# Decoder block on one core: last normalisations of the attention stage moved between engines, scan matmuls reordered

## The reference

```python
x = layernorm(x + mixer(x))          # linear recurrence with a gate
x = layernorm(x + attention(x, ctx)) # 16 heads of 16
x = layernorm(x + experts(x))        # 8 experts, each takes its top 256 tokens

def mixer(x):
    u = x @ W_in + b_in                       # 64 states
    h_t = h_{t-1} @ A + u_t @ Bm              # over 1024 steps
    y = (hs @ C.T + u @ D.T) * sigmoid(x @ W_gate + b_gate)
    return y @ W_out + b_out

def layernorm(x):                             # eps 1e-5
    return (x - mean(x)) / sqrt(var(x) + eps)

def experts(x):
    S = softmax(x @ Wr + br)                  # routing, 8 columns
    # expert e: the 256 tokens with the largest S[:, e]; silu(up), down, times S, summed into the tokens
```

## Time and profile before

| what | value |
|---|---|
| time, median of 3 runs | 288.95 us (288.91 to 289.0) |
| the profiled execution, its own time | 288.22 us |
| its span, first to last instruction | 286.4 us |
| PE busy / DVE / ACT / POOL | 238.1 (83%) / 188.5 (66%) / 152.8 (53%) / 146.1 us (51%) |
| mean granted TensorE clock | 0.923 |

### The profile page before, as it was taken

How to read it: one execution, slowest core, us unless ns; L and a number is a source line. 1 busy time by engine, 2 the same in 40 slices (tenths; PEclk the granted TensorE clock), 3 DMA queues, 4 the chain that set the end, 5 groups by cost and what they waited for, 6 DMA issues and landing times.

```text
span 286.4 us, 5364 instructions
## 1 busy us (share of the span) xinstructions
PE 238.1 (83%) x1833; PEld 180.7 (63%) x1833; DVE 188.5 (66%) x558; ACT 152.8 (53%) x314; POOL 146.1 (51%) x213
## 2 busy tenths in 40 slices
PE   8999999899999899996996111278999999999990
PEld 4765557656566474765674010237999999999880
DVE  0753366456767858697679788753765777775595
ACT  3653612633378763645432377504577879874353
POOL 6859831741524430237388999147782345644000
PEclk9999999999999999999999555556999999999997
DMA  6971040007229192573930069914338664432655
GB/s 187 294 145 39 1 93 21 0 0 169 53 44 208 43 208 52 111 166 89 305 106 2 2 230 367 322 45 109 102 77 241 145 139 89 87 42 33 187 200 220
DMA packets 33676, 35.61 MB, mean 124 GB/s; under 512 B 10610, under 2 KB 25970, under 8 KB 33394
## 3 DMA queue, kind: packets, MB, share of 16 engines
q1 hardware_dynamic: 30130, 30.90, 38.9%
q0 software_dynamic: 2784, 4.00, 8.2%
q10 hardware_dynamic: 736, 0.38, 0.5%
HBM read 18.16 MB, written 8.19 MB: 92 GB/s over the span
## 4 chain that ended last, share of the span: by engine, by line
PE 55%; DVE 21%; ACT 9%; issue 6%; POOL 4%; DMA 3%; DVEq 0%; POOLq 0%; SPq 0%
PE bank L1251 10%; PE bank L1745 6%; PE bank L1448 4%; DVE junk L2109 3%; PE bank L1340 3%; PE bank L1536 3%; PE bank L1500 3%; PE bank L1431 3%; PE bank L1416 2%; PE bank L1509 2%; DVE NMF L1964 2%; PE bank L1489 2%; POOL rstd L839 1%; PE bank L1261 1%; PE bank L1463 1%
## 5 line engine op out<-in xcount | busy, mean ns | idle before, releaser
L911 POOL DMA_INDIRECT summed_rows<-OUT,idx x14 | 26.5, 1890 | 28.0 <-DMA summed_rows<-OUT,idx 21.4
L838 POOL TENSOR_SCALAR var_eps<-mean_var 128x1 f32<-128x1 f32 x32 | 7.3, 227 | 58.8 <-DVE mean_var L1957 58.0
L1251 PE MATMUL bank<-FTH,WUH 128*128 128x256 f32 x94 | 27.3, 291 | 0.0
L1251 PE MATMUL bank<-FTL,WUH 128*128 128x256 f32 x94 | 26.5, 282 | 0.0
L1251 PE MATMUL bank<-FTH,WUL 128*128 128x256 f32 x94 | 26.4, 281 | 0.0
L1168 ACT ACTIVATE bank<-bank,b_up_c 128x256 f32<-128x256 f32 (+1 forms) x48 | 19.5, 446 | 12.7 <-PE bank L1251 12.6
L1745 PE MATMUL bank<-WDH,MH 128*128 128x256 f32 x80 | 23.2, 290 | 1.3 <-DVE ML L2241 1.3
L1964 DVE TENSOR_REDUCE NMF<-bank 128x8 f32<-128x512 f32 x32 | 21.2, 679 | 4.3 <-PE bank L1463 4.3
L901 POOL DMA_INDIRECT XG<-routed_rows,idx x16 | 16.1, 1007 | 13.9 <-DVE idx L2203 9.3
L1745 PE MATMUL bank<-WDH,ML 128*128 128x256 f32 x80 | 22.6, 282 | 0.0
L1745 PE MATMUL bank<-WDL,MH 128*128 128x256 f32 x80 | 22.6, 282 | 0.0
(11 more groups left out here) (357 smaller groups left out, 694.3 us busy)
## 6 DMA issues: line engine op xcount, KB each, us to landing
WDR<-in_L_ffn_W_down SPq DMA_DIRECT2D x8, 640.0 KB
QS<-QH SPq DMA_DIRECT2D x32, 128.0 KB, 2.9
WUR<-in_L_ffn_W_up SPq DMA_DIRECT2D x4, 682.0 KB, 5.2
routed_rows<-X SPq DMA_DIRECT2D x2, 1056.0 KB, 10.3
X<-in_x SPq DMA_DIRECT2D x4, 512.0 KB, 5.1
QS<-QL SPq DMA_DIRECT2D x16, 128.0 KB, 2.8
summed_rows<-X SPq DMA_DIRECT2D x2, 1024.0 KB, 6.0
Y<-summed_rows SPq DMA_DIRECT2D x8, 256.0 KB, 5.7
```

Source lines behind the costliest of these rows:

```text
L911: pool.indirect_dma_start(summed, bass.IndirectOffsetOnAxis(ap=idx[:, 2 * e + h:2 * e + h + 1].bitcast(U32), axis=0), OUT[:, (2 * e + h) % ...
L1251: last = pe.matmul(o, a, b, start=(n == 0), stop=(n == 3 * len(pairs) - 1))
```

## The change

`scale` takes tiles 12, 13 and 14, 15 as pairs: one addition and one power over two columns (`ln_pool` now counts tiles). GpSimd keeps the second normalisation of tiles 0 to 8. For tiles 9 to 15 it makes only the shift, and ScalarE applies it, at three places in its list: tiles 9 to 11 behind the first quarter of `up_high`, 12 and 13 ahead of the exponentials, 14 and 15 behind them. In the recurrence, the next pass's input product is put ahead of `power`, "tw" goes to partitions 64 to 127 of bank 5, so that "pw" and "tw" use different column groups of the array, and the context is turned in the third pass instead of the second.

```diff
-    SECOND_LAST = 6
+    SECOND_BY_ACT = 9
...
-                pool.tensor_tensor(rstd[:, at], var_eps[:, at], neg_half[:, 0:width], ALU.pow).then_inc(ln_pool, 1)
-                scaled[0] += 1
+                pool.tensor_tensor(rstd[:, at], var_eps[:, at], neg_half[:, 0:width], ALU.pow).then_inc(ln_pool, width)
+                scaled[0] += width
...
+            def second_shift(t):
+                k = norm_at[2, t]
+                pool.tensor_scalar(shift[:, k:k + 1], mean_var[:, k, 0:1], rstd[:, k:k + 1], -1.0,
+                                   ALU.mult, ALU.mult).then_inc(ln2_shift, 1)
...
-                for t in Z2_AT.get(g, ()):
-                    scale(norm_at[2, t], shifted=False)
-                for t in Z2_AT.get(g, ()):
-                    if 0 <= t - SECOND_LATER < NT - SECOND_LAST:
+                late = Z2_AT.get(g, ())
+                if late and late[0] >= NT - TPB:
+                    scale(norm_at[2, late[0]], len(late), shifted=False)
+                else:
+                    for t in late:
+                        scale(norm_at[2, t], shifted=False)
+                for t in late:
+                    if 0 <= t - SECOND_LATER < SECOND_BY_ACT:
                         second_normalise(t - SECOND_LATER)
-            for t in range(NT - SECOND_LAST, NT):
-                second_normalise(t)
+                for t in late:
+                    if t >= SECOND_BY_ACT:
+                        second_shift(t)
...
-                act.activation(TW[:, n + 1, :], bank[5][0:NS, 0:NS], ACT.Copy).then_inc(moved[5], 1)
+                act.activation(TW[:, n + 1, :], bank[5][NS:P, 0:NS], ACT.Copy).then_inc(moved[5], 1)
...
+            def second_normalise(t):
+                k = norm_at[2, t]
+                act.wait_ge(ln2_shift, t - SECOND_BY_ACT + 1)
+                act.activation(X[:, t, 0:D], X[:, t, 0:D], ACT.Identity, bias=shift[:, k:k + 1], scale=rstd[:, k:k + 1])\
+                    .then_inc(ln2_out, 1)
+
             up_high(0, 0, 0)
+            for t in range(SECOND_BY_ACT, NT - TPB):
+                second_normalise(t)
             up_high(0, 0, 1)
             up_high(0, 1, 0)
+            second_normalise(NT - TPB)
+            second_normalise(NT - TPB + 1)
             exponentials(0)
             exponentials(1)
+            second_normalise(NT - TPB + 2)
+            second_normalise(NT - TPB + 3)
...
-                    pe.matmul(o[0:NS, 0:NS], own, TW[:, l, :], start=True, stop=True).then_inc(filled[5], 1)
+                    pe.matmul(o[NS:P, 0:NS], own, TW[:, l, :], start=True, stop=True).then_inc(filled[5], 1)
...
-            for j in range(L // 2):
+            def step_inputs(j):
                 o = turn(("step", j))
                 if j > 1:
                     pe.wait_ge(odd_out, j - 1)
-                states = o[:, 0:B * CH]
-                pe.matmul(states, zb_s[NS:P, :], hu4[NS:P, :, 2 * j + 1, :], start=True, stop=False)
+                pe.matmul(o[:, 0:B * CH], zb_s[NS:P, :], hu4[NS:P, :, 2 * j + 1, :], start=True, stop=False)
+
+            step_inputs(0)
+            for j in range(L // 2):
                 if j:
                     wait_moved(pe, ("step", j - 1))
-                pe.matmul(states, ab2_s[:], hu4[:, :, 2 * j, :], start=False, stop=True)\
+                pe.matmul(bank_of(("step", j))[:, 0:B * CH], ab2_s[:], hu4[:, :, 2 * j, :], start=False, stop=True)\
                     .then_inc(sem_filled(("step", j)), 1)
+                if j + 1 < L // 2:
+                    step_inputs(j + 1)
                 power(POWER_AT[j])
                 if j == 1:
-                    scan_constants()
+                    output_weights_turned()
+                if j == 2:
+                    context_turned()
```

More of the change, by code:

```diff
@@ L550, in decoder_block @@
         ln_stats, ln_var, ln_pool, ln_scale = sem("ln_stats"), sem("ln_var"), sem("ln_pool"), sem("ln_scale")
-        ln3_shift, ln1_out, ln2_out = sem("ln3_shift"), sem("ln1_out"), sem("ln2_out")
+        ln3_shift, ln1_out, ln2_out, ln2_shift = sem("ln3_shift"), sem("ln1_out"), sem("ln2_out"), sem("ln2_shift")
         ln3_out, ln3_out_dve, ln3_root = sem("ln3_out"), sem("ln3_out_dve"), sem("ln3_root")
@@ L964, in _ @@
                 wait_filled(act, ("tw", m))
-                act.activation(TW[:, 5 + j, :], bank[5][0:NS, 0:NS], ACT.Copy).then_inc(moved[5], 1)
+                act.activation(TW[:, 5 + j, :], bank[5][NS:P, 0:NS], ACT.Copy).then_inc(moved[5], 1)
                 if j == 1:
@@ L1311, in _, with output_weights_turned @@
                 power(POWERS[n])
-            def scan_constants():
+            def output_weights_turned():
                 pe.wait_ge(cd_in, 32)
@@ L1317, in scan_constants, with context_turned @@
                 last.then_inc(filled[0], 1)
+            def context_turned():
                 pe.wait_ge(kv_in, 80)
```

## The result

The changed kernel takes 290.55 us (median), the kernel before 288.98 in the same comparison; the ratio is 1.0050 (95% interval 1.0029 to 1.0071). The forecast was 287.7. The ratio leaves out one run of 304.72 us, in which the clock was granted less (0.862 on the mean, 0.919 to 0.930 in the other five). The profiled execution of after took 290.04 us, with a span of 288.2; that of before 288.22 and 286.4. The two are compared in what follows.

The account below looks back on a forecast made before the run. GpSimd was taken to bound the attention stage's end (VectorE waits about 1.1 us), PE the step loop. 0.88 + 0.10 + 0.30 = 1.28 us off 288.95 gave 287.7 us; range 287.1 to 288.5 for 8 times in 10.

Parts of the forecast that it names:

- SP and GpSimd behind it: After the attention normalisations: X writes and expert loads some 6 us earlier, GpSimd's weight work earlier; no gain on the path.
- Deviations: End of attention: paired powers and normalisations off GpSimd bring the last deviations at 157.59 instead of 158.47, gaining 0.88 us.
- Second logits instruction: VectorE, last attention block: 0.45 us beside a GpSimd normalisation shortens beside shifts; gain between 0 and 0.25, taken as 0.10.
- The gain of nothing: VectorE's second logits instruction: if GpSimd's shifts collide with it too, no gain there and a sum of 1.18 us.
- ScalarE's seven normalisations: Around the last exponentials: seven at 0.60 us each fit ScalarE's idle times, costing nothing, with 0.15 us to spare.
- Step loop: Recurrence: "tw" overlaps "pw", saving 0.12 us in three passes, taken as 0.30; input order and later context turn give nothing.
- The clock's return stays in its place: Experts' products: they start 1.28 us earlier, full clock does not; 0.64 us lost, 288.3 us; chance 0.20.
- The clock returns late: Experts' products: full clock needs 6.0 us of work, 3.1 us more at half speed, 1.55 lost, 289.2 us; chance 0.07.
- The pairs are no pairs: Attention and loop: power costs every column in full, "tw" waits for "pw"; gain 0.69, 288.3 us; chance 0.12.

Follow-up runs that it names:

- Experiment 1: Changed kernel, with GpSimd's low parts of the first expert weights waiting until VectorE's conversion of the high bits is done: 286.94 us, ratio 0.9934.
- experiment 2: Changed kernel, with the high bits made in PSUM, so that VectorE's conversion reads no SBUF tile; GpSimd's order untouched: 287.47 us, ratio 0.9919.
- experiment 5: Changed kernel, with a GpSimd multiplication by 1 (one SBUF tile in) in front of the low parts' difference: 290.25 us in a single run.
- experiment 6: Kernel before, with GpSimd's low parts of the expert weights made ahead of its six last normalisations instead of behind them: 289.96 us, ratio 1.0056.
- experiment 7: Kernel before, with a GpSimd multiplication by 1 of the raw expert weights ahead of its six last normalisations: 292.35 us in a single run.
- experiment 11: Changed kernel with GpSimd's low parts waiting for VectorE's conversion, run again beside a version with fillers in PE's idle times: 287.1 us, ratio 0.9918.
- the loop alone: Kernel before, with only the recurrence's part of the change (input order, "tw" on partitions 64 to 127, context turned later): 288.19 us, ratio 0.9962.

## Why the prediction was wrong

**The step that failed** is "SP and GpSimd behind it": "GpSimd reaches its weight work earlier as well. Its first gather idles 9.31 us for the indices, so neither pays on the path, and both only widen that cover." It asked of the earlier work only who waits for it, not what it would run beside. It cost 3.21 us. Experiment 1 puts a wait in front of that work alone, and the change gains 1.9 us by the ratio where 1.28 was forecast; experiment 2 leaves the work where it is, moves one operand to PSUM, and the stall is gone as well. The evidence was in the prediction's own rows: the second logits instruction at 0.45 us as a normalisation began and at 0.19 elsewhere. I priced that collision only for the instruction in which I saw it, at 0.25 us at most, and did not ask which other VectorE instruction a GpSimd instruction almost three times as long would meet at its new place. In the same paragraph the loads behind the writes of X were said to come some 6 us earlier: the writes did (159.07, before 165.88), the first load by 0.34 us only (175.29, before 175.63).

The Trainium skill has the rule (SBUF — State Buffer, section SBUF: two separate sides): GpSimd shares a port pair with VectorE, and a VectorE instruction with two SBUF inputs, or one that goes from SBUF to SBUF in a two-port mode, waits when a GpSimd instruction that reads SBUF started first, and the other way round. Experiments 1, 2, 5 and 6 agree: 0.23 us when the conversion is first, 3.44 or 4.13 when it is second, 0.29 when it reads PSUM. That section of the Trainium skill says that the pair is held for the whole instruction; experiment 7, where the sum was done 0.84 us before GpSimd's multiplication, and the conversion of the kernel before inside a normalisation do not agree.

**The other steps.**

- *Deviations, 0.88 us.* Measured 2.04 - 1.21 = 0.83. The power over two columns takes 0.71 us, so the second column adds 0.14 where I took 0.19; but the pair starts 0.08 us behind the mean's end. VectorE's wait fell from 1.15 to 0.32 us, about as said.
- *Second logits instruction, 0.10 us.* It got the whole 0.25: the shifts beside it, one column each, did not hold it (0.19 us at 157.09). The gain of nothing, which the prediction had for the case that they collide, did not come.
- *ScalarE's seven normalisations, nothing.* Right. In the changed kernel ScalarE stood 0.27 us before the first exponentials and 0.98 us before the second, each time for VectorE, and in experiment 1 the first counts start at 160.08 and 160.16 on the two engines, as the conversion allows.
- *Step loop, 0.30 us.* The pairs gave 0.33, and the order, costed at nothing, 0.19: I had counted instructions and not what stands next to what. With the context's new place 0.57 in all.
- *Rivals.* The return of the clock did move against the products, as "The clock's return stays in its place" allows, but it did not stay: the products came 1.36 us later and the return 2.54 us later. "The clock returns late" came true in part: 4.17 us behind the products instead of 2.99, which cost 0.56 us, short of the 5.5 us that it needed to turn the sum. None of the rivals held the stall, which made the loss. ("The pairs are no pairs" leaves 0.79 us with the 0.10 of the logits in it, not 0.69.)

Put together: -0.57 (loop) - 0.83 - 0.25 + 3.21 + 0.56 = +2.12 us; with the 0.22 that the profiled execution was ahead when the loop began, +1.90, against 290.04 - 288.22 = 1.82 measured.

Without the collision the change is worth 0.57 + 0.83 + 0.25 = 1.65 us by the trace. The versions of experiments 1, 2 and 11 measured ratios of 0.9934, 0.9919 and 0.9918, that is 1.9 to 2.4 us; the loop alone measured 1.1 us with an interval from 0.7 to 1.6, for 0.57 in its trace. The rest is not accounted for. The return of the clock differs between executions by enough to hide it, but that was not shown.

## What to carry to other kernels

When a change frees an engine, list what that engine will now do earlier and lay it against the other engines' timeline at its new place, even if nobody waits for it. For a long GpSimd instruction that reads SBUF (3.42 to 4.14 us here) look for VectorE instructions that read two SBUF tiles or copy from SBUF to SBUF on the path; put one operand in PSUM (experiment 2) or let the long instruction wait for the short one (experiment 1). A row whose duration differs between two places is a warning for the whole kernel, not for that row alone.

## What had not been expected of the hardware

- A 128x128 conversion on VectorE can last 4.13 us instead of 0.23, and a few hundredths of a us in the order of two starts decide it (0.23 us when it started 0.003 us ahead of GpSimd in experiment 6, 3.44 when it started 0.05 us behind in the changed kernel).
- The 128-row state product takes 0.63 us to the next start behind a product of 64 rows and 0.53 behind one of 128. For the 64-row inputs the rows agree less: they start 0.31 us behind the turned context, where a 128-row product starts 0.22 behind it, but take about 0.63 us themselves behind either kind (23.41 to 24.04 behind the context, 21.20 to 21.82 behind "tw", both before). What sets it was not tried.
- The return to full clock does not keep its distance to the first expert product: 2.99 us before, 4.17 after, 5.8 with the loop alone (products from 194.08; 0.53 granted from 198 to 200, so full clock at about 199.9), at much the same work. In eight of the 13 profiles it keeps another distance, 40.96 us behind the point at which the clock fell at the end of the attention stage (157.20 to 198.16 before, 158.91 to 199.87 with the loop alone, 158.10 to 199.06 in experiment 11, by the traces' records of the clock); in the changed kernel it is longer, and why is open. The Trainium skill (TensorE: Matmul & The Clock Gate, section What's actually happening) has the activity window run freely, not reset when a kernel starts. Distances to the products that change from run to run are what that lets one expect; no run here shows the window itself.
